# Identity products in three gaps of TensorE between the recurrence and the expert selection of a decoder kernel

## What is computed

```python
x = _layernorm(x + _L1_attn_ref(x, ...))            # the recurrence, a scan over 256 steps
x = _layernorm(x + _L1_xattn_ref(ctx_1024, x, L1_xattn_Wq))
x = _layernorm(x + _L1_ffn_ref(x, ...))             # expert selection and 64 experts

def _L1_xattn_ref(enc_outputs, x, Wq):
    q = einsum('bld,hd->blh', x, Wq)
    k = einsum('bld,hd->blh', enc_outputs, Wq); v = k
    scores = where(causal, einsum('bqh,bkh->bqk', q, k) / sqrt(128), -inf)
    return einsum('bqk,bkh->bqh', softmax(scores), v)

def _route(x, router_w, e_bias):                     # in _L1_ffn_ref
    scores = sigmoid(x @ router_w.T)                 # then 4 of 8 groups, 8 experts of 64
```

## Time and profile before

| | us |
|---|---|
| median of 3 runs | 1085.94 |
| lowest and highest | 1085.79, 1091.52 |
| the profiled execution | 1087.3 |
| its span, first to last instruction | 1085.5 |
| TensorE matmuls busy | 959.6 (88%) |
| VectorE, ScalarE, GpSimd busy | 778.1, 586.0, 421.4 |
| mean granted TensorE clock | 0.922 of full |

### The profile page before, as it was taken

The page is one execution under the profiler, slowest core; times in us unless marked ns, Lnnn a source line. Parts: engine busy times, 40 slices in busy tenths (PEclk is TensorE's granted clock), DMA queues, the critical chain, the costliest instruction groups (busy, mean ns, idle before and its releaser), DMA issues.

```text
span 1085.5 us, 17936 instructions
## 1 busy us (share of the span) xinstructions
PE 959.6 (88%) x5387; PEld 802.4 (74%) x5387; DVE 778.1 (72%) x2002; ACT 586.0 (54%) x1375; POOL 421.4 (39%) x490
## 2 busy tenths in 40 slices
PE   6999999999997799995884768887979999999994
PEld 5899999999984557773663658785657888888883
DVE  4666666666668672441788999935759999999995
ACT  3666666666656632444575333324656555555554
POOL 3566666666654412554540747643381000000001
PEclk8999999999998698997897688886989999999998
DMA  6232323222314101341101222001006666566551
GB/s 245 72 103 89 100 82 106 82 99 87 109 65 155 40 10 28 85 79 49 30 20 40 78 79 78 1 1 45 14 1 162 173 173 165 171 180 175 165 145 39
DMA packets 46979, 98.29 MB, mean 91 GB/s; under 512 B 7106, under 2 KB 23170, under 8 KB 45779
## 3 DMA queue, kind: packets, MB, share of 16 engines
q1 hardware_dynamic: 44466, 92.64, 27.8%
q0 software_dynamic: 2464, 5.05, 2.4%
HBM read 75.25 MB, written 22.41 MB: 90 GB/s over the span
## 4 chain that ended last, share of the span: by engine, by line
PE 42%; issue 19%; POOL 18%; DVE 15%; ACT 4%; DMA 1%; SPq 1%; POOLq 0%; DVEq 0%; ACTq 0%
PE PS L1783 8%; PE PS L1784 8%; PE PS L1785 8%; POOL P L661 7%; POOL WS L670 3%; PE PS L1979 3%; DVE r0b L1589 3%; POOL WS L666 2%; DVE rb L1602 2%; PE PS L1993 2%; PE PS L1928 1%; PE PS L2135 1%; PE PS L1934 1%; DVE dfb L1594 1%; ACT Xp L443 1%
## 5 line engine op out<-in xcount | busy, mean ns | idle before, releaser
L661 POOL TENSOR_TENSOR P<-P,rl 128x256 f32<-128x256 f32 (+1 forms) x130 | 104.8, 827 | 121.2 <-DVE rl L1220 121.2
L436 POOL TENSOR_TENSOR rs<-ms,neghalf 128x4 f32<-128x4 f32 (+1 forms) x28 | 26.0, 928 | 304.1 <-DVE nm L430 303.9
L1213 DVE CUSTOM_DVE_ANT_0 P<-PS,cmask 128x128 f32<-128x128 f32 (+1 forms) x260 | 77.1, 352 | 70.6 <-issue 70.5
L1138 ACT ACTIVATE FG<-PS 128x512 f32<-128x512 f32 x112 | 67.0, 598 | 103.3 <-PE PS L1785 103.3
L882 ACT ACTIVATE P<-P,mn 128x128 f32<-128x128 f32 (+1 forms) x260 | 114.3, 444 | 1.9 <-DVE mn L1213 1.9
L1783 PE MATMUL PS<-XTh,W 128*128 128x512 f32 x256 | 102.3, 399 | 0.8
L1784 PE MATMUL PS<-XTl,W 128*128 128x512 f32 x256 | 101.1, 395 | 0.0
L1785 PE MATMUL PS<-XTh,W 128*128 128x512 f32 x256 | 101.1, 395 | 0.0
L1854 PE MATMUL PS<-VO,PT 128*128 128x128 f32 x804 | 100.6, 275 | 0.0
L1854 PEld LDWEIGHTS PS<-VO,PT 128*128 128x128 f32 x804 | 95.0, 192 | 0.0
L1769 DVE TENSOR_TENSOR FU<-FG,PS 128x512 f32<-128x512 f32 x112 | 77.0, 688 | 23.3 <-PE PS L1785 23.3
(11 more groups left out here) (449 smaller groups left out, 2660.7 us busy)
## 6 DMA issues: line engine op xcount, KB each, us to landing
GI<-coef SPq DMA_DIRECT2D x56, 256.0 KB, 4.1
GW<-coef SPq DMA_DIRECT2D x56, 256.0 KB, 4.1
w3s<-WS SPq DMA_DIRECT2D x32, 384.0 KB, 2.6
W<-w3s SPq DMA_DIRECT2D x32, 384.0 KB, 3.3
Wb<-decay SPq DMA_DIRECT2D x7, 1024.0 KB, 4.6
WR<-in_w SPq DMA_DIRECT2D x32, 192.0 KB, 2.5
WR<-in_w SPq DMA_DIRECT2D x16, 256.0 KB, 2.8
w12f<-WS SPq DMA_DIRECT2D x16, 256.0 KB, 2.1
```

The lines of the kernel that those rows point to most:

```text
L661: last = pool.tensor_tensor(v, v, f, ALU.mult)
L1138: act.activation(FG[:, k % 2, :], bank(4 + k % 2), ACT.Silu).then_inc(sem("fg_done"), 1)
L1213: dve.tensor_tensor_reduce(out=P[:, slot, c:c + w], in0=scores(par, q), in1=cmask[:, 256 - w:256], scale=1.0, scalar=3e38, op0=ALU.add, op ...
```

## The change

A helper `keep_clock(n, b)` issues n plain products of the identity with itself into the first 128 columns of bank b, with no wait and no increment. Nobody reads them. It is called three times: ten products into bank 7 after the transposes of chunks 0 and 1 of norm 3, twenty into bank 7 after the last context scores, five into bank 0 after the weighted sums. The call of `in_turn` is written out as a loop so that the first call fits in; the order of the other instructions stays as it was. No other engine's compute or DMA instruction moves.

```diff
-            in_turn(lambda c: ln_transpose(pe, 3, c), context_scores, 1)
+            def keep_clock(n, b):
+
+                for _ in range(n):
+                    pe.matmul(bank(b)[:, 0:128], ident[:, :], ident[:, :], start=True, stop=True)
+
+            for c in range(2):
+                ln_transpose(pe, 3, c)
+            keep_clock(10, 7)
+            context_scores(0)
+            for c in range(2, NC_):
+                ln_transpose(pe, 3, c)
+                context_scores(c - 1)
+            context_scores(NC_ - 1)
+            keep_clock(20, 7)
             for t in range(T):
                 pe.wait_ge(sem("e_prob"), t // 8 + 1)
...
                 if c % 2:
                     logits_by_token(c // 2)
 
+            keep_clock(5, 0)
             in_turn(lambda c: ln_transpose(pe, 4, c), router_step, 2)
             residual()
```

## The result

| | before | changed |
|---|---|---|
| median of 15 runs, us | 1088.29 | 1084.26 |
| lowest and highest | 1084.97, 1091.52 | 1081.68, 1085.60 |
| profiled execution, span | 1085.5 | 1082.9 |
| mean granted clock | 0.922 | 0.927 |

The ratio is 0.9964, with a 95% interval of 0.9951 to 0.9977: 3.9 us less, 2.5 to 5.3. The interval leaves out 1, so the gain is clear of noise, although it is smaller than the 0.5% that the prediction took for the least that a measurement can tell. A later comparison of the same two kernels gave 0.9956 (0.9941 to 0.9970), 4.8 us. Ratios here are given as measured; they are not the quotient of the two medians beside them and differ from it by up to 0.001.

What follows compares the result with a forecast made beforehand. No single engine bounds the whole program; TensorE holds 42% of the chain, and two of its blocks there run at low clock. Terms 2.47 + 1.39 + 0 = 3.9 us, off 1085.94, give 1082.0 us, range 1078.5 to 1087.0.

Steps and rivals of the forecast that it cites:

- scores block: Context scores and eight transposes after the ten products: 4.56 us at full clock instead of 7.03, saving 2.47 us.
- probabilities' block: 16 probability transposes and first four weighted sums after the twenty: 3.04 us at full clock instead of 4.43, saving 1.39.
- third part: Five products behind the weighted sums, 1.2 us long: no cost and no gain, router products within 0.6 us either way.
- second term: The 1.39 us saving in the probabilities' transposes and first weighted sums, bought by the twenty products.
- Covers: Waits hiding the fillers: ten end about 0.9 us early in 3.27 us idle, twenty 0.57 us early in 5.37 us.
- The signs: Clock 1.00 from 726 to about 750, transposes waiting for GpSimd, VectorE's first addition about 744.2, later steps 3.9 us sooner.
- the forecast itself: Whole kernel: a gain of 2.8 to 5.2 us, giving 1080.7 to 1083.1 us; chance 0.60.
- Rival 2: Residual behind the router also slow in typical runs of before: 2.6 us more, gain 6.5 us, 1079.4 us; chance 0.18.
- Rival 3: Ten fail to hold the clock, twenty run slow and end late: 1.2 to 2.8 us slower; chance 0.08.
- Rival 4: The 16 probability transposes stay at the low clock, 3.33 us: gain only 2.5 us, 1083.5 us; chance 0.06.
- Rival 5: Gain given back later as work shifts against the clock's changes: 0 to 1.5 us left, 1084.4 to 1085.9; chance 0.08.
- After norm 4: Next norm and first router products: the clock falls there as before, since TensorE is mostly idle; zero gain taken.

Runs made afterwards that it cites:

- forty_for_twenty: Changed kernel with forty products instead of twenty after the context scores; ratio 0.9966 to the kernel before, median 1086.11 us.
- before_again: The kernel before, unchanged, run against itself for a second profile; ratio 0.9999, median 1087.99 us.
- twenty_only: Changed kernel with only the twenty products after the context scores, without the ten and the five; ratio 0.9991 to the kernel before, median 1089.17 us.
- as_transposes: Changed kernel with each identity product replaced by two float32 transposes of the identity; ratio 0.9949 to the kernel before, median 1084.32 us.
- scan_and_norm: Changed kernel plus seven products ahead of the weights' product at the recurrence's end and products between norm 4's transposes; ratio 0.9957 to the kernel before, median 1083.39 us.
- both_filled: Changed kernel plus products between norm 4's transposes and in the gaps ahead of the gates' transposes; ratio 0.9960 to the kernel before, median 1083.80 us.
- ten_only: Changed kernel with only the ten products after the first eight norm 3 transposes; ratio 0.9977 to the kernel before, median 1087.32 us.

## Why the prediction was right, and where not

- **The sum.** Predicted 3.9 us, by the ratio 3.9; the trace has 3.67 and the second comparison 4.8, so that the two figures are equal is luck, while the mechanism is the one forecast. The terms in the trace: scores block 4.63 us against 4.56 predicted (saved 2.40 for 2.47), probabilities' block 3.16 against 3.04 (1.27 for 1.39), third part 0 for 0. The 0.12 us that the second term fell short is in the 16 transposes, 2.06 us in the chain where I had 1.92, and it is not their price: in forty_for_twenty, where they wait for nothing, they take 1.91. The rest is the wait between the two halves of the softmax. GpSimd's second half ends at 742.97, and the ninth transpose's weights are loaded only at 743.02, after an idle of 0.20. I had put that wait at hundredths; it costs 0.15 us.
- **Covers.** The ten ended 1.03 us early (0.9 predicted), the twenty 0.86 (0.57 predicted: the 20 products end 4.5 us behind the last score, not 4.8). Forty instead of twenty showed that this slack is real and that what goes past it is nearly all paid (2.7 us in the medians for 3.35 in the stretches).
- **The signs.** The clock was 1.00 from 727.7 to 752.8; the transposes waited for GpSimd; VectorE's first addition came at 745.21, 17.52 us behind the start of the stretch where it had been 21.18; and the residual came 3.67 us sooner behind that start. The shift of all later steps held to the residual; behind it this pair of profiles lost 0.3 us.
- **The absolute time** was 2.3 us too low: 1082.0 against 1084.26. That is within the range but outside the 1080.7 to 1083.1 of the forecast itself. The step that failed is the base. I subtracted from the median of three runs, 1085.94; fifteen runs have their median at 1088.29. The profiled execution of 1087.3 would have led to 1083.4, and the median of fifteen to 1084.4. Rival 2 rested on the right observation, that before leaves to chance which matmuls come out slow, but it asked for the residual to be hit; what before_again shows is slow scores (8.57 us) and partly slow sums, with the residual at full clock (3.84 us). So the typical gain seems to be above the one that a single cheap profile gives: 4.9 us by the mean of the two stretches of before, 3.9 and 4.8 by the two timings. The forecast's own range, 2.8 to 5.2, covers both.
- **Rival 3**, slower, did not come: the clock stayed at 1.00 over the gap. twenty_only shows that its mechanism exists, with 0.5 us of lateness where the ten are missing.
- **Rival 4**, slow transposes, is refuted by the changed kernel itself (clock 1.00, 2.06 us); as_transposes shows further that transposes can even be the filler.
- **Rival 5**, a gain given back later, did not come for this change, but did for two that went further: scan_and_norm through VectorE, and both_filled, as far as one pair of traces shows, through a DMA.
- **After norm 4** the clock fell and the router's first products ran at 0.50, as forecast; filling that gap too is worth 0.24 us in one trace and did not hold the clock in another.

## What to carry to other kernels

Where TensorE waits for others and its next block is on the chain, products without readers in the wait can make that block run at the full clock, as long as they end before the wait does; here they cost 0.24 us each at the full clock and by estimate 0.45 at the low one (the 16 weighted sums of ten_only, all at 0.50, took 7.19 us; the 0.40 of the prediction was a row that changed clock on the way). Place the first filler where the clock is still full. Fill only ahead of blocks whose saved time has nothing close behind it: look for the next wait (VectorE's scan, the weights' DMA) before counting the gain. And take the base from several profiles, since one of the kernel before may show the cheap case.

## What the runs showed of the hardware

- The same program took 25.28 and 27.55 us from norm 3 to norm 4, with the waits for other engines equal (3.27 and 5.38 us) and the whole difference in rows of TensorE while the granted clock was 0.50 for longer; with the gaps filled eight traces had 21.61 to 21.64.
- Products of the identity with itself, nearly all zeros, held the granted clock at 1.00 over the waits, and so did float32 transposes of the identity, 0.11 us each (40 in 4.54 us).
- At the low clock TensorE can be busy without a break and the clock not come back for a while: in twenty_only scores, transposes and then fillers ran unbroken from 731.3 to 742.8 at 0.50, and the clock was 1.00 from 743.0. In the first profile of before the same scores had it back after 5 us, at 736.4.
